# A quantised feed-forward kernel: yq as float16 multiples, w2 rounded on POOL, half-width dummy products

## What is computed

```python
U = (mu @ W_dec + b_dec).reshape(B, 257, K)
param = einsum('bik,kj->bij', U, V)
y = einsum('bsd,bde->bse', x, param[:, :-1]) + param[:, -1][:, None]

def quant_weight(w):            # ternary, one scale for the matrix
    s = clip(mean(abs(w)), EPS)
    return clip(round(w / s), -1, 1) * s
def quant_act(x):               # one scale for each row
    scale = 127 / clip(max(abs(x), axis=-1), EPS)
    return clip(round(x * scale), -128, 127) / scale

h = gelu(quant_act(y) @ quant_weight(w1).T)
out = x + quant_act(h) @ quant_weight(w2).T
```

## Time and profile before

| | us |
|---|---|
| median of 3 runs | 68.99 |
| lowest and highest | 68.6 and 71.72 |
| the profiled execution | 68.6 |
| its span (first to last instruction) | 66.8 |
| mean granted TensorE clock in it | 1.000 |

### The profile page before, as it was taken

One profiled execution on the slowest core, in us unless ns is written; L12 is line 12 of the kernel. 1 busy time (PEld: TensorE's weight loads), 2 busy tenths in 40 slices (PEclk: granted clock), 3 DMA queues, 4 the chain that ended last, 5 costly groups with the idle time before them and its releaser, 6 DMA issues.

```text
span 66.8 us, 1289 instructions
## 1 busy us (share of the span) xinstructions
PE 57.9 (87%) x449; PEld 30.0 (45%) x449; DVE 45.1 (67%) x92; ACT 35.8 (54%) x52; POOL 28.5 (43%) x47
## 2 busy tenths in 40 slices
PE   2999999998896799989977959999999999969920
PEld 0325332122332363433513533755849467959800
DVE  2000708565328784899999698599897989996530
ACT  3506006600067297999987644766959393852000
POOL 6400001000000108997939795376493929960000
PEclk9999999999999999999999999999999999999999
DMA  0899999999999999700099959979699969824062
GB/s 0 225 363 417 398 426 418 414 391 386 416 412 427 432 412 427 294 25 0 0 189 59 218 118 194 174 141 182 125 264 181 157 208 309 320 96 157 0 235 79
DMA packets 18342, 16.18 MB, mean 242 GB/s; under 512 B 14752, under 2 KB 15136, under 8 KB 17952
## 3 DMA queue, kind: packets, MB, share of 16 engines
q1 hardware_dynamic: 18192, 15.86, 79.6%
q10 hardware_dynamic: 144, 0.24, 1.5%
HBM read 10.47 MB, written 2.10 MB: 188 GB/s over the span
## 4 chain that ended last, share of the span: by engine, by line
PE 38%; DMA 20%; DVE 15%; SPq 9%; ACT 8%; issue 4%; POOL 2%; DVEq 0%
DMA w_dec_all<-in_w_dec_dram 16%; PE ps_h L463 14%; PE ps_o L483 8%; PE ps_z L483 7%; SPq L249 5%; ACT w_dec_all L607 4%; DMA yq_t<-yq_h 4%; DVE pair_max L713 3%; DVE h_max L731 3%; PE ps_y L435 3%; DVE o_sb L755 3%; SPq L266 2%; PE ps_z L423 2%; POOL hq_h L370 2%; ACT y_q L596 2%
## 5 line engine op out<-in xcount | busy, mean ns | idle before, releaser
L370 POOL TENSOR_SCALAR hq_h<-w_dec_all,pair_rcp 128x1024 f16<-128x1024 f32 x14 | 15.7, 1118 | 7.9 <-DVE pair_rcp L727 7.9
L463 PE MATMUL ps_h<-w_t,yq_t 128*128 128x512 bf16 x64 | 16.0, 380 | 1.2 <-DMA yq_t<-yq_h 0.7
L713 DVE TENSOR_REDUCE pair_max<-w_dec_all 128x2 f32<-128x2048 f32 x7 | 15.9, 2276 | 0.0
L607 ACT ACTIVATE w_dec_all<-ps_h,pair_c 128x1024 f32<-128x1024 f32 x10 | 10.9, 1112 | 6.4 <-PE ps_h L463 6.4
L398 PE MATMUL ps_h<-warm_h 128*128 128x512 bf16 x39 | 13.2, 459 | 1.3 <-POOL warm_h L308 1.3
L463 PEld LDWEIGHTS ps_h<-w_t,yq_t 128*128 128x128 bf16 x64 | 5.5, 98 | 8.6 <-issue 1.3
L483 PE MATMUL ps_o<-w_t,hq_t 128*128 128x256 f16 x64 | 8.3, 273 | 0.6 <-DVE o_sb L755 0.5
L483 PE MATMUL ps_z<-w_t,hq_t 128*128 128x256 f16 x64 | 8.3, 272 | 0.0
L579 ACT ACTIVATE w_abs<-w_sb 128x1024 f32<-128x1024 f32 (+1 forms) x3 | 2.7, 914 | 9.1 <-DMA w_sb<-in_w_tr_dram 9.0
L398 PEld LDWEIGHTS ps_h<-warm_h 128*128 128x128 bf16 x39 | 3.8, 119 | 7.8 <-issue 5.9
L483 PEld LDWEIGHTS ps_o<-w_t,hq_t 128*128 128x128 f16 x64 | 6.0, 98 | 2.6 <-DVE o_sb L755 0.7
(11 more groups left out here) (83 smaller groups left out, 68.8 us busy)
## 6 DMA issues: line engine op xcount, KB each, us to landing
w_sb<-in_w_tr_dram SPq DMA_DIRECT2D x4, 512.0 KB, 8.7
x_sb<-in_x_dram SPq DMA_DIRECT2D x2, 1024.0 KB, 19.0
out_dram<-o_sb SPq DMA_DIRECT2D x7, 256.0 KB, 2.9
w_dec_all<-in_w_dec_dram SPq DMA_DIRECT2D x3, 512.0 KB, 7.5
w_dec_all<-in_w_dec_dram SPq DMA_DIRECT2D x3, 448.0 KB, 8.2
x_t<-in_x_tr_dram SPq DMA_DIRECT2D x1, 1024.0 KB, 16.7
w_dec_all<-in_w_dec_dram SPq DMA_DIRECT2D x1, 576.0 KB, 10.3
x_t<-in_x_tr_dram SPq DMA_DIRECT2D x2, 256.0 KB, 10.9
```

What stands on the lines that cost most here:

```text
L370: pool.tensor_scalar(hq_h[n % NB][:, :], h_tile(n), scale, UNIT, ALU.mult, ALU.mult).then_inc(hq_ready, 1)
L463: last = nc.tensor.matmul(ps_h[k][:, half, :], yq_t[:, p, n % 2, c, :], w1_t[:, c, half * HALF:(half + 1) * HALF], start=(c == 0), stop=(c ...
L607: nc.scalar.activation(h_tile(n), ps_h[n % 2][:, :, :].rearrange("p a n -> p (a n)"), ACT.Gelu, scale=c1_of(n)).then_inc(gelu_done, 1)
L713: nc.vector.tensor_reduce(pair_max[:, p, 2:4], h_pair[p % NH], AXX, ALU.max, apply_absolute_value=True).then_inc(pair_max_ready, 1)
```

## The change

It has six parts.

1. yq as float16 multiples of 2^-24. The scale of y now holds 1/UNIT (`1.0 / (QMAX * UNIT)` in y_scales, pair_scales and h_scales), ACT writes y_q as float16 with no bias, `yq_t` and `w1_t` are float16, and the two copies out of PSUM become plain int16 copies. PE transposes y_q itself with the float16 identity; the bfloat16 identity goes.
2. `narrow_y` is gone with its buffer: SP's transpose_yq(4 to 6) reads y_q and waits for ACT's yq_ready; quantise_y(6) and (7) on ACT wait for the landing of the transposes of yq4 and yq5 instead of for narrow_y.
3. UNIT moves from POOL's multiplication of h into the scale; POOL's pass stays one with two operations (times scale, times 1.0), the DVE half of the last tile (L810) becomes one with one operation.
4. `factor` on POOL is gone: DVE's scale operation (L668) writes both columns of `s12` itself.
5. w2 is rounded on POOL alone. Rounding now has two operations (times 1/s, min 1.0), the clip becomes max -1.0, times 1.0. ACT's pass between gelu(1) and quantise_y(2) is gone. POOL's list is round_w2(0), scale_y(2), round_w2(1), clip_w2(0), clip_w2(1).
6. Each dummy product is two of 128 x 256.

```diff
-        w1_t = sb("w1_t", [P, DC, H], BF16)
+        w1_t = sb("w1_t", [P, DC, H], FP16)
-        y_q = [sb(f"y_q{k}", [P, 2, D]) for k in range(2)]
-        yq_h = [sb(f"yq_h{k}", [P, 2, D], BF16) for k in range(2)]
-        yq_t = sb("yq_t", [P, NP, 2, DC, P], BF16)
+        y_q = [sb(f"y_q{k}", [P, 2, D], FP16) for k in range(2)]
+        yq_t = sb("yq_t", [P, NP, 2, DC, P], FP16)
...
             def transpose_yq(p):
-                sp.wait_ge(yqh_ready, p - 3)
-                sp.dma_start_transpose(yq_t[:, p, :, :, :].rearrange("p t c q -> p (t c) q"),
-                                       yq_h[p % 2][:, :, :].rearrange("p t c -> p (t c)")).then_inc(yqt_landed[p % 2], 16)
+                sp.wait_ge(yq_ready, 2 * p + 2)
+                sp.dma_start_transpose(yq_t[:, p, :, :, :].rearrange("p t c q -> p (t c) q"), yq_flat[p % 2]).then_inc(yqt_landed[p % 2], 16)
...
-            def factor(k, ready):
-                pool.wait_ge(ready, 1)
-                pool.tensor_scalar(s12[:, 2 * k:2 * k + 2], s_w[:, k:k + 1].broadcast_to([P, 2]), (1.0, 1.0 / UNIT)[k], None,
-                                   ALU.mult).then_inc(s_s12[k], 1)
...
-            def narrow_y(p):
-                pool.wait_ge(yq_ready, 2 * p + 2)
-                if p >= 6:
-                    pool.wait_ge(yqt_landed[p % 2], yqt_count(p - 2))
-                pool.tensor_scalar(yq_h[p % 2][:, :, :].rearrange("p t c -> p (t c)"),
-                                   y_q[p % 2][:, :, :].rearrange("p t c -> p (t c)"), 1.0, -MAGIC,
-                                   ALU.mult, ALU.add).then_inc(yqh_ready, 1)
...
             def round_w2(n):
                 pool.wait_ge(s_s2, 2)
-                pool.tensor_scalar(part_of(w2_r, n), part_of(w2_sb, n), s_rcp[:, 1:2], None, ALU.mult).then_inc(s_w2r[n], 1)
+                pool.tensor_scalar(part_of(w2_r, n), part_of(w2_sb, n), s_rcp[:, 1:2], 1.0, ALU.mult, ALU.min).then_inc(s_w2r[n], 1)
             def clip_w2(n):
                 pool.wait_ge(s_w2r[n], 1)
-                pool.tensor_scalar(part_of(w2_t, n), part_of(w2_r, n), 1.0, -1.0, ALU.min, ALU.max).then_inc(s_w2q[n], 1)
+                pool.tensor_scalar(part_of(w2_t, n), part_of(w2_r, n), -1.0, 1.0, ALU.max, ALU.mult).then_inc(s_w2q[n], 1)
...
-                pool.tensor_scalar(hq_h[n % NB][:, :], h_tile(n), scale, UNIT, ALU.mult, ALU.mult).then_inc(hq_ready, 1)
-
-            factor(0, s_s1)
+                pool.tensor_scalar(hq_h[n % NB][:, :], h_tile(n), scale, 1.0, ALU.mult, ALU.mult).then_inc(hq_ready, 1)
+
             for p in range(AHEAD - 1):
                 scale_y(p)
+            round_w2(0)
+            scale_y(AHEAD - 1)
             round_w2(1)
-            factor(1, s_s2)
-            scale_y(AHEAD - 1)
             for n in range(2):
                 clip_w2(n)
             for p in range(PAIRS):
                 quantise_h(2 * p)
                 scale_pair(p)
-                if 1 <= p < LATE_Y - AHEAD:
-                    narrow_y(p + AHEAD)
                 quantise_h(2 * p + 1)
...
             def keep_warm(n):
-                for _ in range(n):
-                    nc.tensor.matmul(ps_idle, warm_h[:, 0:P], warm_h[:, :], start=True, stop=True)
+                for _ in range(2 * n):
+                    nc.tensor.matmul(ps_idle[:, 0:256], warm_h[:, 0:P], warm_h[:, 0:256], start=True, stop=True)
...
             def quantise_y(p):
                 if p >= 6:
-                    act.wait_ge(yqh_ready, p - 5)
+                    act.wait_ge(yqt_landed[p % 2], yqt_count(p - 2))
...
                     nc.scalar.activation(y_q[p % 2][:, i, :], y_of[p][:, i, 0:D], ACT.Copy,
-                                         bias=MAGIC, scale=scale).then_inc(yq_ready, 1)
+                                         scale=scale).then_inc(yq_ready, 1)
...
-                nc.scalar.activation(yq_t[:, p, :, :, :].rearrange("p t c q -> p (t c) q"), ps_yqt[n].bitcast(I16), ACT.Copy,
-                                     bias=-OFFSET).then_inc(yqt_copied, 1)
+                nc.scalar.activation(yq_t[:, p, :, :, :].rearrange("p t c q -> p (t c) q").bitcast(I16),
+                                     ps_yqt[n].bitcast(I16), ACT.Copy).then_inc(yqt_copied, 1)
...
             gelu(1)
-            act.wait_ge(s_s2, 2)
-            round_w(w2_r[:, 0:HC // 2, :].rearrange("p t c -> p (t c)"), w2_sb[:, 0:HC // 2, :].rearrange("p t c -> p (t c)"),
-                    s_rcp[:, 1:2], s_w2r[0])
             quantise_y(2)
...
-                nc.vector.tensor_scalar(s_w[:, k:k + 1], w_all[:, k:k + 1], 1.0 / (H * D), EPS,
+                nc.vector.tensor_scalar(s12[:, 2 * k:2 * k + 2], w_all[:, k:k + 1].broadcast_to([P, 2]), 1.0 / (H * D), EPS,
                                         ALU.mult, ALU.max).then_inc(ready, 1)
...
-                copy_q(yq_t[:, p, i0:i1, :, :].rearrange("p t c q -> p (t c) q"), ps_yqt[n]).then_inc(yqt_copied, 1)
+                nc.vector.tensor_copy(yq_t[:, p, i0:i1, :, :].rearrange("p t c q -> p (t c) q").bitcast(I16),
+                                      ps_yqt[n].bitcast(I16)).then_inc(yqt_copied, 1)
...
-            nc.vector.tensor_scalar(hq_h[(NT - 1) % NB][:, 0:HALF], h_tile(NT - 1)[:, 0:HALF], h_rcp[:, NT - 1:NT], UNIT,
-                                    ALU.mult, ALU.mult).then_inc(last_hq[0], 1)
+            nc.vector.tensor_scalar(hq_h[(NT - 1) % NB][:, 0:HALF], h_tile(NT - 1)[:, 0:HALF], h_rcp[:, NT - 1:NT], None,
+                                    ALU.mult).then_inc(last_hq[0], 1)
```

More of the change, by code:

```diff
@@ L13 @@
 P = 128
-OFFSET = 16384.0
-MAGIC = 1.5 * 2 ** 23 + OFFSET
 UNIT = 2.0 ** -24
@@ L100, in adaln_ffn @@
         w_all = sb("w_all", [P, 2])
-        s_w = sb("s_w", [P, 2])
         s12 = sb("s12", [P, 4])
@@ L136, in adaln_ffn, with blocks @@
         ps_z = pb("ps_z", [P, 512])
[L138 to L144, removed]
+        def blocks(bank, n):
+            return bank[:, 0:n * P // 2].bitcast(FP16).rearrange("p (c q) -> p c q", c=n)
+        yq_flat = [y_q[k][:, :, :].rearrange("p t c -> p (t c)") for k in range(2)]
         ps_u = [ps_y[:, 0, :], ps_y[:, 1, :], ps_h[1][:, 0, :], ps_h[1][:, 1, :], ps_o]
@@ L160, in adaln_ffn @@
         late_bank = {LATE: ps_y, LATE + 1: ps_h[0], LATE + 2: ps_y, LATE + 3: ps_h[1]}
-        ps_hqt = {n: [blocks(late_bank[n][:, half, :], HC // 2, FP16) for half in range(2)] for n in late_bank}
+        ps_hqt = {n: [blocks(late_bank[n][:, half, :], HC // 2) for half in range(2)] for n in late_bank}
         o_of = [(ps_o, ps_z)[n % 2][:, 0:D] for n in range(NT)]
@@ L190, in adaln_ffn @@
         s_s2 = sem("w2_scale_ready")
-        s_s12 = [sem(f"w{k + 1}_factor_ready") for k in range(2)]
         s_w1r = [sem(f"w1_rounded{a}") for a in range(DC)]
@@ L326, in scale_y @@
                 if p == 0:
-                    pool.wait_ge(s_s12[0], 1)
+                    pool.wait_ge(s_s1, 1)
                 pool.tensor_tensor(c1[:, p, :], y_inv[:, p, :], s12[:, 0:2], ALU.mult).then_inc(c1_ready, 1)
@@ L334, in scale_pair @@
                 if p == 0:
-                    pool.wait_ge(s_s12[1], 1)
+                    pool.wait_ge(s_s2, 1)
                 pool.tensor_tensor(pair_c[:, p, cols], pair_inv[:, p, cols], s12[:, cols], ALU.mult).then_inc(pair_c_ready, 1)
-            def narrow_y(p):
-                pool.wait_ge(yq_ready, 2 * p + 2)
-                if p >= 6:
-                    pool.wait_ge(yqt_landed[p % 2], yqt_count(p - 2))
-                pool.tensor_scalar(yq_h[p % 2][:, :, :].rearrange("p t c -> p (t c)"),
-                                   y_q[p % 2][:, :, :].rearrange("p t c -> p (t c)"), 1.0, -MAGIC,
-                                   ALU.mult, ALU.add).then_inc(yqh_ready, 1)
             def part_of(w, n):
@@ L389, in _ @@
             pool.wait_ge(hqt_landed[(NT - 1 - NB) % LAG], 16 * ((NT - 1 - NB) // LAG + 1))
-            pool.tensor_scalar(hq_h[(NT - 1) % NB][:, HALF:], h_tile(NT - 1)[:, HALF:], h_rcp[:, NT - 1:NT], UNIT,
+            pool.tensor_scalar(hq_h[(NT - 1) % NB][:, HALF:], h_tile(NT - 1)[:, HALF:], h_rcp[:, NT - 1:NT], 1.0,
                                ALU.mult, ALU.mult).then_inc(last_hq[1], 1)
@@ L443, in transpose_yq @@
                 for c in range(DC * i0, DC * i1):
-                    last = nc.tensor.transpose(ps_yqt[n][:, c - DC * i0, :], yq_low[p % 2][:, c * P:(c + 1) * P], ident_h[:, :])
+                    last = nc.tensor.transpose(ps_yqt[n][:, c - DC * i0, :], yq_flat[p % 2][:, c * P:(c + 1) * P], ident_f[:, :])
                 last.then_inc(yqt_done, 1)
@@ L492, in transpose_hq @@
                 if n == LATE:
-                    pe.wait_ge(s_identf, 1)
                     pe.wait_ge(yqt_copied, len(YQT_PARTS))
@@ L530, in _ @@
             keep_warm(4)
-            pe.wait_ge(s_identh, 1)
+            pe.wait_ge(s_identf, 1)
             transpose_yq(0)
@@ L656, in _ @@
         def _(dve):
-            def copy_q(dst, src):
-                return nc.vector.tensor_scalar(dst, src.bitcast(I16), -OFFSET, None, ALU.add)
```

(10 more changed lines are left out.)

4 lines of the change are left out of this document (removed).

## The result

| | before | after |
|---|---|---|
| median of 4 runs each, us | 69.59 | 79.5 |
| lowest and highest, us | 68.6 and 71.72 | 78.06 and 80.42 |
| profiled execution and its span, us | 68.6, 66.8 | 78.06, 76.0 |
| mean granted TensorE clock | 1.000 | 0.955 |

The ratio is 1.140, with a 95% interval of 1.113 to 1.168. The forecast was no change (68.7, range 67.8 to 69.8); the change costs 14%. Executions of one and the same kernel fall into faster and slower ones (before: 68.6 to 71.72), so a ratio compares the faster ones alone, while a median takes in all.

A forecast was written before the change was run, and what follows sets the result against it. The prediction saw a chain of waits: w_dec's loading to 17 us, small steps, then PE from 39.94. From 68.6 us, terms of -0.03 and +0.02 left 68.6; allowing for the 68.99 median it took 68.7, range 67.8 to 69.8.

The forecast's parts named there:

- the price of the new POOL passes: POOL's two roundings of w2: 1.12 us each, hidden behind DVE's work on pair 0, so the cost is nothing.
- the two clips to 30.85: POOL's clips of w2 behind the roundings: taken at 2.04 us for both, ending at 30.85, before quantise_h(0)'s scale comes.
- quantise_h(0) starts at 25.31 + 2r + 0.2 + 2.04: On POOL: start of quantise_h(0) if each rounding of w2 takes r us; 31.0 as before was expected.
- some 1.0 us of lateness: Delay of quantise_h(0) on POOL that idle time ahead of hq2's transpose on SP would swallow: some 1.0 us.
- each 0.1 costs 0.2: On POOL: once a rounding of w2 takes over r = 2.2 us, each further 0.1 us costs 0.2.
- the dummies at 0.02 us: PE's halved dummy products: same columns, 0.02 us for weight loads at three places, between 0 and 0.15.
- A: Rival on POOL: writing int16 is what is slow, both roundings take 2.82 us, 69.6 us in all; chance 0.15.
- B: Rival on PE: halved dummies let the clock fall between 20 and 26 us, 3.5 us more, 72; chance 0.05.
- C: Rival on the chain: ACT's pass over w2 comes off in full, 1.0 us, giving 67.6; chance 0.08.
- D: Rival on ACT: float16 passes or int16 copies slow by 0.1 us at some five links, 69.1; chance 0.06.
- ACT's pass: Removing ACT's rounding of w2 before quantise_y(2): 0.06 us left there, 0.03 us gained overall, as DVE comes next.
- narrow_y's going: Three POOL passes of 0.62 us removed: worth 0, as SP's queue still issues yq4 right behind hq2.

The follow-up runs named there:

- e4_probes: The kernel before with twelve extra POOL passes of 128 x 512 on scratch, of various operations and types, in POOL's idle time: 68.91 us.
- e2: The changed kernel with only the clip put back to min, max; rounding keeps times 1/s, min 1.0: 73.83 us in one run.
- e1: The changed kernel with both operations of each POOL pass of one kind (rounding mult, mult; clip min, max): 71.31 us, ratio to before 1.030.
- e7: The kernel before with a second dummy product of 8 columns behind each full-width dummy: 69.97 us, ratio to before 1.014.
- e6: The kernel before with dummy products of half the width, their number not doubled: ratio to before 0.999.
- e3: The kernel before with only the dummy products halved in width and doubled in number: four runs, 69.41 to 70.97 us.
- e11: The changed kernel with only the dummy products back at full width: 77.84 us in one run.
- e8: The kernel before with all of w2's rounding on POOL as mult, mult and ACT's pass over w2 gone: ratio to before 0.999.
- e5: The changed kernel with POOL's operation pairs of one kind and the dummy products at full width: 69.36 us, ratio to before 1.001.
- e9: e5 with the transpose of yq4 ahead of that of hq2 on SP's queue: 69.32 us in 12 runs, ratio to before 0.995.

## Why the prediction was wrong

**The step that failed is the price of the new POOL passes.** The prediction took bounds of 1.02 and 2.82 us for the rounding and chose 1.12, because "the odd one is the count of operations". The count does matter (1.50 alone against 0.61 in e4_probes), so the reading of L351 was right. But the rows of before did not show the rest: of the pairs measured, only those whose operations are of one kind are cheap. All two-operation rows of before are such pairs: (mult, mult), (mult, add), (min, max). The new (mult, min) took 3.71, outside the range of what had been thought possible.

**The clip was priced at nothing without being looked at.** The prediction wrote "the two clips to 30.85" with the duration of (min, max), although part 5 of the change makes them (max, mult). They rose from 1.02 to 3.63 us each: 5.2 of the 9.0 us on POOL, and against the forecast as much as the roundings. An operation that the diff rewrites is a new form, even where its types and place are unchanged.

**The schedule behind the price was right.** "quantise_h(0) starts at 25.31 + 2r + 0.2 + 2.04", with r = 3.68 and the clips' real 7.23 in place of 2.04, gives 40.1, which with the 1.34 of the ladder is the 41.4 measured. The "some 1.0 us of lateness" to be swallowed were 1.0 (10.38 at quantise_h(0), 9.34 at yq4's issue). That "each 0.1 costs 0.2" beyond r = 2.2 is borne out in direction only, by e2 (one run) against e1.

**The second failed step is the one that costed the dummies at 0.02 us.** It counted columns and weight loads and left out that instructions are themselves loaded by the DMA engines. "The dummies of the first 17 us lie beside the loading" held for PE's time and not for its instructions: 78 instructions more (39 products and as many weight loads) moved a fetch from 20.5 to 16.4 us, and PE waited 1.03 us for x_t. The price of the count by itself is 1.4% (e7). That the count does it is shown (e6, e7); that it does so through the packet is argued.

**Rivals.** A (int16 is what makes POOL slow, 69.6) is wrong in its cause: (mult, mult) into int16 takes 0.62 for 512 columns. B (the clock falls for the halves) is wrong in its cause too: e3 has the halves and a clock of 1.00, e11 has none and 0.932; in the changed kernel and in e11 it fell while PE waited for hq0. C is wrong (e8). D never showed: e5 is at 1.001.

**What held.** ACT's pass was worth nothing (e8). (Of it the prediction had 0.06 us left for quantise_y(2); there was none, since that pass starts 0.09 to 0.10 us behind the reciprocal with and without ACT's pass.) narrow_y's going moved nothing, because SP's order kept yq4 behind hq2 (e9). The float16 forms cost nothing in sum (e5).

The Trainium skill, "GPSIMD Engine Reference", section 3.1, has a body of up to two operations bound by the ports at 1.03 cycles an element, from which the prediction estimated 0.9 us for 1024 columns. The traces roughly agree for pairs of one kind (1.02 to 1.12 us) and for none of the others: 2.85 for one operation, 3.63 to 3.71 for a pair of two kinds.

## What to carry to other kernels

A POOL `tensor_scalar` is cheap here with two operations that are both arithmetic or both comparisons; give a single one a second (times 1.0), and don't fold a clamp into a scaling. Price each instruction that a diff rewrites by a row of exactly its operations. Where no row has them, let the range go past the dearest row known. Instructions added to one engine are also a transfer: look at where the instruction fetches fall against the loads that the chain waits for.
